# Feed-forward front, normalisation and q/k/v projections of a macaron layer reworked, with three waits moved

## What is computed

```python
x = x + 0.5 * ffn(_layernorm(x))
x = x + attn(_layernorm(x))
x = x + 0.5 * ffn(_layernorm(x))

def ffn(x):      # 8 experts of width 64, 2 chosen by row; a shared MLP of width 128
    logits = xf @ gate_w.T + lb_bias
    topw, topi = top_k(sigmoid(logits), 2); topw = topw / (topw.sum(-1) + 1e-8)
    for e in range(8):
        m = topi == e
        wmean = (topw * m).sum() / maximum(m.sum(), 1)
        out = out + where(m.any(-1)[:, None], _mlp(xf, e) * wmean, 0)
    return out + _mlp(x, shared)          # _mlp: silu(x @ gw.T) * (x @ uw.T) @ dw.T

def attn(x):     # 16 heads of 8, 4 key/value heads, causal, with a linear bias by position
    q, k, v = x @ Wq + bq, x @ Wk + bk, x @ Wv + bv
    return softmax(q @ k.T * scale + slopes * rel) @ v @ Wo + bo
```

## Time and profile before

| | |
|---|---|
| Median of 3 runs (lowest, highest) | 827.32 us (825.87, 828.84) |
| The profiled execution's own time | 826.89 us |
| Its span, first to last instruction | 824.9 us |
| Mean granted TensorE clock | 0.96 of 2.4 GHz |
| Busy: PE, DVE, ACT, POOL | 753.1, 592.5, 431.5, 69.7 us |
| Chain that ended last, shares | PE 63%, DVE 19%, issue 12%, ACT 3%, POOL 1% |

### The profile page before, as it was taken

How to read it: one execution, slowest core, us unless ns; L and a number is a source line. 1 busy time by engine, 2 the same in 40 slices (tenths; PEclk the granted TensorE clock), 3 DMA queues, 4 the chain that set the end, 5 groups by cost and what they waited for, 6 DMA issues and landing times.

```text
span 824.9 us, 15805 instructions
## 1 busy us (share of the span) xinstructions
PE 753.1 (91%) x5508; PEld 329.2 (40%) x5508; DVE 592.5 (72%) x1913; ACT 431.5 (52%) x626; POOL 69.7 (8%) x83
## 2 busy tenths in 40 slices
PE   3979998775799999999999999999998879899998
PEld 2623333332234344444444444444443655233343
DVE  4875332777899999999999999999993377433301
ACT  3432323333337687676876768767677434223211
POOL 2200000444400000000000000000000021000000
PEclk9979999999769999999999999999999989699999
DMA  4201000153401010110101101011000000000012
GB/s 128 67 0 15 0 1 0 49 160 95 133 13 34 20 34 18 34 35 22 32 18 35 34 21 32 18 35 35 22 14 2 1 1 1 0 1 0 0 39 64
DMA packets 33068, 26.08 MB, mean 32 GB/s; under 512 B 5707, under 2 KB 32331, under 8 KB 32997
## 3 DMA queue, kind: packets, MB, share of 16 engines
q1 hardware_dynamic: 32996, 25.15, 10.7%
HBM read 14.62 MB, written 10.26 MB: 30 GB/s over the span
## 4 chain that ended last, share of the span: by engine, by line
PE 63%; DVE 19%; issue 12%; ACT 3%; POOL 1%; SPq 0%; DMA 0%; DVEq 0%; ACTq 0%; POOLq 0%
PE ps L964 57%; DVE mx L853 8%; PE ps L969 5%; DVE xn L659 3%; DVE mx L846 1%; ACT h_all L580 1%; POOL rstd L421 1%; DVE stats L647 1%; PE ps L1012 1%; DVE x L802 1%; DVE h_all L846 1%; DVE mv L651 1%; DMA x<-in_x 0%; SPq L310 0%; DVE wb L874 0%
## 5 line engine op out<-in xcount | busy, mean ns | idle before, releaser
L580 ACT ACTIVATE h_all<-ps 128x1024 f32<-128x1024 f32 (+3 forms) x384 | 291.1, 811 | 118.4 <-PE ps L964 115.0
L853 DVE TENSOR_REDUCE mx<-ps 128x1 f32<-128x512 f32 (+2 forms) x352 | 222.6, 681 | 8.5 <-PE ps L964 5.9
L964 PE MATMUL ps<-ks,xnT_all 57*128 57x512 bf16 (+3 forms) x768 | 180.3, 336 | 10.7 <-DVE mx L846 5.3
L964 PE MATMUL ps<-h_all,vb 128*32 128x512 f32 (+3 forms) x1536 | 163.0, 498 | 0.6 <-ACT osb L569 0.6
L964 PE MATMUL ps<-xnT_all,ks 59*128 59x512 bf16 (+3 forms) x768 | 158.4, 330 | 3.7 <-ACT h_all L580 3.4
L846 DVE CUSTOM_DVE_ANT_0 h_all<-ps,mask_w 128x384 bf16<-128x384 f32 (+1 forms) x256 | 148.9, 618 | 2.1 <-issue 0.3
L670 DVE TENSOR_TENSOR h_all<-ps,sg 128x512 f32<-128x512 f32 (+1 forms) x80 | 55.1, 689 | 107.9 <-PE ps L964 71.3
L964 PEld LDWEIGHTS ps<-ks,xnT_all 57*128 57x128 bf16 x768 | 56.7, 94 | 141.3 <-DVE mx L846 66.1
L964 PE MATMUL ps<-cb 64*128 64x64 bf16 (+3 forms) x1216 | 111.8, 214 | 0.0
L495 ACT ACTIVATE sg<-ps 128x512 f32<-128x512 f32 x80 | 47.6, 598 | 106.3 <-PE ps L964 106.3
L964 PEld LDWEIGHTS ps<-cb 64*128 64x128 bf16 x1216 | 79.8, 96 | 16.7 <-issue 0.3
(11 more groups left out here) (123 smaller groups left out, 627.3 us busy)
## 6 DMA issues: line engine op xcount, KB each, us to landing
xnT_all<-q_scr SPq DMA_DIRECT2D x64, 96.0 KB
q_scr<-qp SPq DMA_DIRECT2D x8, 384.0 KB, 2.7
ks<-k_scr SPq DMA_DIRECT2D x64, 48.0 KB
x<-in_x SPq DMA_DIRECT2D x8, 256.0 KB, 2.9
q_scr<-qp SPq DMA_DIRECT2D x8, 256.0 KB, 2.9
out<-x SPq DMA_DIRECT2D x8, 256.0 KB, 2.3
xnT_all<-bias_scr SPq DMA_DIRECT2D x64, 18.0 KB
q_scr<-qp SPq DMA_DIRECT2D x8, 128.0 KB, 2.3
```

Of the source, the lines that this page charges most:

```text
L580: act.activation(pr[:, (NSTEP * i + s) % PR_BUFS, p:HPG:SLOTS, lo:HALF], ps[:, b:b + 2, lo:HALF], ACT.Exp)\
L853: dve.tensor_reduce(m, src, AX.X, V.max).then_inc(a_out, 1)
L964: return pe.matmul(o, l, r, start=start, stop=stop, skip_group_check=True)
```

## The change

- **Loops.** Every group and batch loop is written out; the hardware loops are gone.
- **Loads.** x of groups 0 and 1 first, then wg and wu, then the other x loads without a wait between them. The small loads (ident, gate_w, lb, rank) go on ACT's queue. The masks, esel, slopes and qpos come later under `s_const`; ACT's conversion of them moves to behind group 6 of the first front, DVE's slope parts to behind the choice.
- **Normalised rows.** DVE writes a shift, -mean times rstd, in one small operation; ACT writes xn in four ACTIVATEs with scale and bias columns (24 groups in all).
- **Front.** One copy of the transposes in place of two. The shared expert of groups 4 to 7 (`LATE_SHARED`) is done behind the last gate on PE, behind the sigmoid on ACT, and within the choice on DVE. The mask transposes of group 0 come ahead of the first two expert tiles. maskT and esel have 128 rows, zeros below the eighth.
- **Projections.** v is projected straight into rows (four matmuls with xnT as weights, 32 columns), k into four 32-partition blocks of 128 columns (four matmuls with 32-column weights); `v_T` is gone. k's split moves from POOL to DVE, on 128 x 128. SP stores k with six DMAs in place of three (nine in all for each group).
- **Order.** `xn_T` is issued behind `down` instead of within it; DVE takes the values of group c-1 in place of c-2.

```diff
-STORES = 2 * len(RUNS)
+STORES = len(RUNS) + PARTS
+LATE_SHARED = GROUPS - 4
 def over_groups(body):
+    for c in range(GROUPS):
+        body(c, c % 2, c == 0, c == GROUPS - 1)
...
-                    sp.dma_start(k_scr[b, :, r:r + products, n], kp[:, par, 0:products]).then_inc(dw, 16)
+                    for m in range(products):
+                        sp.dma_start(k_scr[b, :, r + m, n].rearrange("k (t n) -> t k n", t=GT), kp[:, par, m])\
+                            .then_inc(dw, 16)
...
+            def ln_apply(c, par, s_nm, s_T, s_xn):
+                act.wait_ge(s_nm, c + 1)
+                after(act, s_T, c)
+                for t in range(GT):
+                    ins = act.activation(xn[:, t, :], x[:, c * GT + t, :], ACT.Identity, bias=shift[:, par, t:t + 1],
+                                         scale=rstd[:, par, t:t + 1])
+                ins.then_inc(s_xn, 1)
...
                 def front(c, par, first, last):
                     act.wait_ge(f.T, c + 1)
-                    after(act, f.U, c - 1)
-                    act.activation(xnT[:, par, :], bank(7 * par), copy).then_inc(f.xT, 1)
                     act.activation(xnT_all[:, c, :], bank(7 * par), copy).then_inc(f.xA, 1)
-                    if not first:
+                    if not last:
+                        ln_apply(c + 1, 1 - par, f.nm, f.T, f.xn)
+                    if 0 < c <= LATE_SHARED:
                         silu(c - 1, 1 - par)
+                    if load_constants and c == GROUPS - 2:
+                        constants()
...
                 act.wait_ge(f.lg, GROUPS)
                 act.activation(sc, lg, ACT.Sigmoid).then_inc(f.sig, 1)
+                for c in range(LATE_SHARED, GROUPS):
+                    silu(c, c % 2)
...
                     if qkv and not first:
                         qk(c - 1, 1 - par)
+                    if qkv:
+                        ln_apply(c, par, f.nm2, f.Tb, f.xn2)
...
+            def ln_shift(c, par, s_rs, s_xn, s_nm):
+                after(dve, s_xn, c - 1)
                 dve.wait_ge(s_rs, c + 1)
-                for t in range(GT):
-                    ins = dve.tensor_scalar(xn[:, t, :], x[:, c * GT + t, :], mv[:, par, t, 0:1],
-                                            rstd[:, par, t:t + 1], V.subtract, V.mult)
+                dve.scalar_tensor_tensor(out=shift[:, par, :], in0=mv[:, par, :, 0], scalar=-1.0, in1=rstd[:, par, :],
+                                         op0=V.mult, op1=V.mult).then_inc(s_nm, 1)
...
                     if not last:
                         statistics(c + 1, 1 - par)
-                    ln_apply(c, par, f.rs, f.T, f.xn)
+                    ln_shift(c, par, f.rs, f.xn, f.nm)
                     if c >= 2:
                         finish(c - 2, par)
...
                     mm(bank(5), wq[:, :], xnT[:, par, :]).then_inc(f.Q, 1)
-                    mm(ps[0:2 * KVH * DH, 6, :], wkv[:, :], xnT[:, par, :]).then_inc(f.K, 1)
+                    for t in range(GT):
+                        ins = mm(ps[:, 7, w * t:w * t + w], xnT[:, par, t * P:(t + 1) * P], wkv[:, w:2 * w])
+                    ins.then_inc(f.V, 1)
+                    for t in range(GT):
+                        ins = mm(ps[w * t:w * t + w, 6, 0:P], wkv[:, 0:w], xnT[:, par, t * P:(t + 1) * P])
+                    ins.then_inc(f.K, 1)
```

More of the change, by code:

```diff
@@ L206, in macaron @@
         rstd = sb("rstd", [P, 2, GT])
+        shift = sb("shift", [P, 2, GT])
         idle = sb("idle", [P, 4 + HPG])
@@ L265, in macaron @@
         s_late = sem("s_late")
-        s_x0 = sem("s_x0")
+        s_const = sem("s_const")
+        s_x = [sem(f"s_x{c}") for c in range(GROUPS)]
         s_init = sem("s_init")
@@ L373, in _ @@
                 load_stack(1, 1, 1, half)
-            with sp.Fori(1, BATCH) as b:
+            for b in range(1, BATCH):
                 store_parts(2 * b, b, 0)
@@ L396, in _ @@
             od = out.rearrange("(c t p) f -> c p t f", t=GT, p=P)
-            with sp.Fori(0, GROUPS) as c:
+            for c in range(GROUPS):
                 sp.wait_ge(f2.x, c + 1)
@@ L422, in rsqrt @@
                 pool.wait_ge(rs_sem, c + 1)
[L424 to L434, removed]
-                if not first:
-                    split(c - 1, 1 - par)
-            over_groups(pool, lambda c, par, first, last: rsqrt(c, par, f1.ve, f1.xn, f1.rs))
+            over_groups(lambda c, par, first, last: rsqrt(c, par, f1.ve, f1.xn, f1.rs))
             clear_keys()
             pool.wait_ge(f1.U, HT * GROUPS)
-            over_groups(pool, down_body)
-            split(GROUPS - 1, 1)
+            over_groups(lambda c, par, first, last: rsqrt(c, par, f1.ve2, f1.xn2, f1.rs2))
             pool.wait_ge(s_late, 16 * len(late_loads))
@@ L469, in _ @@
             pool.wait_ge(o_bo, BO_PARTS)
-            over_groups(pool, lambda c, par, first, last: rsqrt(c, par, f2.ve, f2.xn, f2.rs))
+            over_groups(lambda c, par, first, last: rsqrt(c, par, f2.ve, f2.xn, f2.rs))
         @block.scalar
@@ L475, in _, with constants @@
             copy = ACT.Copy
[L476 to L479, removed]
+            for dst, name in small_loads:
+                act.dma_start(dst[:, :], dram[name]).then_inc(s_small, 16)
+            def constants():
+                act.wait_ge(s_init, 2)
+                act.wait_ge(s_const, 16 * len(const_loads))
+                act.activation(cb[:, :, :], c128[:, 0:7 * P].rearrange("p (a n) -> p a n", n=P), copy).then_inc(s_cb, 1)
+                act.activation(mask_w[:, HALF - P:HALF], c128[:, 7 * P:8 * P], copy)
+                act.activation(esel[0:EXPERTS, :], esel_f[:, :], copy).then_inc(s_cb, 1)
             def stack_constants():
@@ L708, in choose, with shared @@
                 def choose():
+                    def shared(c):
+                        hidden(c, c % 2, c, MT)
                     dve.wait_ge(f.sig, 1)
@@ L717, in choose @@
                     mask(0, 0)
+                    for c in range(LATE_SHARED + 2, GROUPS):
+                        shared(c)
                 def mask(c, par):
@@ L942, in out_proj @@
                 residual(1, 1)
-                with dve.Fori(1, BATCH - 1) as b:
+                for b in range(1, BATCH - 1):
                     gather(2 * b + 2, b + 1, 0, 0)
@@ L1032, in routed_tiles, with down @@
                             .then_inc(f.tops, 1)
-                over_groups(pe, front)
-                up(GROUPS - 1, 1, MT, xnT[:, 1, :], None)
-                pe.wait_ge(f.xA, GROUPS)
-                over_groups(pe, routed_tiles)
+                over_groups(front)
+                for c in range(LATE_SHARED, GROUPS):
+                    up(c, c % 2, MT, xnT_all[:, c, :], None)
+                pe.wait_ge(s_cb, 2)
+                over_groups(routed_tiles)
             def ffn_down(f, qkv):
-                def down(c, par, transpose=0):
+                def down(c, par, transpose=False):
                     after(pe, f.yT, c - 1)
                     for i in range(HT):
-                        if transpose > 1 and i == 2:
-                            v_T(c - 3)
-                        if transpose and i == HT // 2 + 1:
-                            xn_T(c - 2)
                         ins = mm(bank(par), wds[:, i, :], h_all[:, c, i, :], start=(i == 0), stop=(i == HT - 1))
                     ins.then_inc(f.Y, 1)
+                    if transpose:
+                        xn_T(c - 2)
                 def project(c, par):
@@ L1069, in body @@
                     if not last:
-                        down(c + 1, 1 - par, 0 if first or not qkv else 1 if isinstance(c, int) and c == 1 else 2)
+                        down(c + 1, 1 - par, qkv and not first)
                     pe.wait_ge(f.yT, c + 1)
```

190 lines of the change are left out of this document (86 added, 104 removed).

## The result

The kernel after takes **807.78 us** (median of 4 runs, 805.28 to 809.99), beside 827.25 for the kernel before on the same chip: a ratio of 0.976, 95% interval 0.973 to 0.980. The prediction said 813.5, within 804 to 823, and faster at 0.86. Number and side were right, the number in part by luck: the reasons held only in part, and the largest term of the result had been priced at nothing.

A forecast was written before the change was run, and what follows sets the result against it. It saw the first down stage bound by a loop through xn and POOL's k split, the fronts by PE. First step -1.4, down stage -11.8, second step -0.3 summed to -13.5, giving 813.5 us, range 804 to 823.

The forecast's parts named there:

- choice and clock: Choice and experts: choice -1.2, third tile +1.8, then -3.3 and -5.8 in the two steps if the clock holds.
- the fronts: Both fronts: a new loop of 4.4 a group for 3.1; +1.3 at the first last gate, +4.9 in the second step.
- the down stage: First down stage: period 8.0 against 10.3, ending xn's wait and POOL's slowing; -14.3 to the last residual add.
- attention: From the last residual add to the first scores: DVE's added work and the wait for k cost +2.5.
- The failed step: Experts: 128 rows instead of 8 in the mask matmul change nothing, since its columns set the time.
- the slowing by POOL: First down stage: DVE's four xn take 3.79 while POOL splits k, 1.11 where POOL did nothing; this ends.
- the one SP stall: First down stage: SP's stores are late once, holding ACT's queue, so PE stalls 2.5 once.
- if the shorter idle keeps the clock: -3.3 and -5.8: Experts, third tile to group 2's mask transposes: 9.6 at 2.4 GHz, where it took 12.9 and 15.4.
- the rival of the clock at the front's end: Front's end: the clock drops and shared tiles run partly at 1.2 GHz; 3.6 a step, 821 us; chance 0.17.
- POOL holding the shift: Fronts: POOL's rsqrt delays DVE's shift by 1.0 us for each of eight groups; 822 us; chance 0.12.
- k's stores: Down stage: k stores bound SP, deciding against the kernel from about 1.3 each; 837 us at 1.5; chance 0.04.
- The early loop: Fronts: the loop closes earlier and the period stays 3.1, eight groups less 1.3; 804 us; chance 0.08.

The follow-up runs named there:

- e1: The changed kernel with the mask matmul back on 8 rows of weights and mask: 823.63 us, ratio 0.994 to the kernel before.
- e11: The kernel before, with only k's three split operations moved from POOL to DVE: 821.57 us, ratio 0.991.
- e7: The changed kernel with DVE writing xn in the down stage, ACT still in the fronts: 805.28 us, ratio 0.972 to the kernel before.
- e6: The changed kernel with silu(c-1) ahead of xn(c+1) in ACT's front: 805.01 us, ratio 0.971 to the kernel before.
- e10: The changed kernel with DVE writing all xn and the shared tiles of groups 4 to 6 back in the front: 790.96 us, ratio 0.953 to the kernel before.

## Why the prediction was right, and where it wasn't

By the spans of the profiled executions the two kernels differ by -16.8; the sum of the prediction was -13.5. (By the medians it is -19.5.) In the two expert stretches the mask matmul brings -16.3 that I didn't have (-8.0 and -8.3, after against e1). The other steps miss by +13.0 together: choice and clock +4.1 and +3.3 (e1 against before: +1.4 and -1.9, where I had -2.7 and -5.2), the fronts +0.5 and +1.2, the down stage +0.7, attention +3.5, the end -0.3. The two nearly cancel, and that is luck. The kernel that I had priced, with the mask's columns alone setting its time, is e1: 823.63, just past the far end of the range, and worth 0.6%, not 1.6%. (e1's attention is 4.2 shorter than the changed kernel's, so the steps other than the mask miss by 9.1 there.)

- **The failed step: "128 rows instead of 8 in the mask matmul: nothing, its columns set the time."** The columns set its duration in the record, not what its neighbours lose. The starts in the kernel before already showed it: the gate matmul takes 0.86 to the next start with a full matmul behind it (726.52 to 727.38) and 0.96 with the mask behind it (724.29 to 725.25). From the mask to the next matmul it is 0.31, and 0.22 with 128 rows (716.07 to 716.29). My own sum held the price too: a tile of 2.25 less four instructions of 0.43 leaves 0.53 for a mask matmul that I had put at 0.2 one sentence earlier. I priced the instruction and didn't read the gaps around it.
- **Down stage: size right (-13.6 for -14.3), cause half right.** I named two things, the wait for xn and the slowing by POOL. e11 and e7 show that only POOL's k split mattered: with it gone DVE has room for xn, and everything else in the stage together adds 1.8 of 13.6. The estimates of xn on ACT (1.6; 1.65), the period (8.0; 7.91) and the one SP stall (2.5; PE 3.3) held. The terms of PE's work add up to 7.6, not 7.5, which changes nothing here.
- **Fronts: right.** +1.8 and +6.1 for +1.3 and +4.9, a period of 4.44 for 4.4, with the chain that was read from the two queues; e6 opened it where it was said to close. First transposes at 9.05 for 9.1. In the second step the transposes of group 3 come 14.0 behind the first ones where 13.0 was worked out; its terms add up to +4.8, not +4.9.
- **Choice and clock: the clock right behind the choice, the time wrong.** The clock after the choice was kept (1.00 in 52 to 60, for 0.55 before), as "if the shorter idle keeps the clock: -3.3 and -5.8" asks. It was lost ahead of it: 0.50 from 23.0 to 29.8 and from 33.2 to 46.9, for 1.00 before. This was the rival of the clock at the front's end, at 0.17, and half of it came true beside the forecast, not in place of it. From the gate's end to the mask transposes it takes 9.6 and 8.9 where 7.9 was worked out: DVE's two multiplies in the choice wait 1.8 and 1.1 for shared matmuls that ran at 1.2 GHz. The tiles themselves end in time; PE waits 0.27 for the mask. From there to the third tile it takes 4.9 as worked out (4.95). The larger miss lies behind that: to the mask transposes of group 2 it takes 11.7 and 10.3, for 9.6 by PE's work alone, at a clock of 1.00. In the first step DVE is the bound there. Windows view of that stretch, after:

```profile
56.79:68.53 11.74, 9.42 (x26) 3.44 (x26) 11.28 (x23) 3.42 (x6) 0.00 (x0) 1.00 0.00 0
```

PE waits 1.37 of it for DVE's multiply and 0.80 for the mask; the same stretch takes 11.7 in e1, with 8 rows. The stretch before held 11.94 of DVE's work (52.73 to 65.62), which I hadn't added up. e10 shows that the move of the shared tiles is worth nothing once xn is on DVE.

- **Attention: +6.0 for +2.5.** First scores came 35.3 behind the last add for 31.7, +3.6 for the +2.5. Windows view from the last add to the first scores, before and then after:

```profile
205.43:237.14 31.71, 25.89 (x82) 7.85 (x82) 28.99 (x96) 6.66 (x10) 10.07 (x10) 0.66 0.31 95
```
```profile
186.98:222.32 35.34, 29.34 (x105) 11.39 (x103) 28.53 (x99) 7.79 (x15) 2.64 (x4) 0.50 0.29 85
```

The other 2.3 lie between the first scores and the last add of attention's output (427.6 for 425.3), which no edit touches. They go with the granted clock, a mean of 0.98 for 0.99: 1.00 is reached 8.9 us behind the first scores, for 3.1 before. In e1 that part takes 423.5.

All the other kernels take 458.8 to 463.1 for the attention, in their profiled executions, where the kernel before took 457.0. What picks the value within that span isn't settled: no kernel was tried that keeps PE busy across ACT's wait for the store, behind which the clock fell in the changed kernel (wq's two instructions at 180.73 take 2.08, the price of 1.2 GHz).
- **Rivals that fell.** POOL holding the shift: DVE's shift took 0.16, and POOL's rsqrt starts behind it (24.28 and 24.50), not ahead. The rule of the Trainium skill's page "SBUF — State Buffer" ("SBUF: two separate sides") therefore wasn't tested on the shift: the two didn't meet. Where xn met k's split they took turns (last section), as such a lock would have it; xn beside the rsqrt shows none. k's stores: 0.50 to 0.66 each, far from 1.3. The early loop, which I put at 804, is 813.4 less 10.4, so 803.0. Loops written out: no stretch shows anything of it, but nothing was run with that alone.

## What to carry over

Read the starts of the neighbours of a small matmul, not its duration: one whose weights have 64 rows or fewer, or 8 columns, between full ones costs 0.2 to 0.3 more than its columns, and zeros up to 128 make that vanish for a memset. Before work is moved off an engine because that engine waits or runs slowly, find what slows it: moving the small disturber (k's split off POOL) did nearly all of what moving the large victim (xn to ACT) was meant to do, and the move of the victim cost 16 us, 13.6 of it in the fronts, where the other engine's queue closed a loop. Price each stretch by every engine's work in it: behind the choice PE had 9.6 and DVE over 11. When a total comes out as forecast, still cut both traces at the same events; here the cut showed errors of 13 and 16 that hid each other by luck.

## What the hardware showed that I had not expected

- A bf16 matmul with few rows between fp32 ones of 128 costs 0.30, with a step between 64 and 96 rows: 8 and 64 rows cost the same (2.23 from gate to gate), 96 and 128 the same (1.93). Below the step the weight loads beside it aren't hidden behind the matmul ahead. Width does the like: 8 columns for 128 cost 0.2 for each set of transposes.
- Three wide POOL operations of 1.15 beside DVE turned four xn of 1.11 into 3.79; the four-element rsqrt beside the same xn didn't. They don't share, they take turns: the first three xn operations end 0.09 behind one POOL operation each (159.84, 160.95 and 162.17, for POOL's 159.75, 160.86 and 162.08), and the fourth, alone, takes 0.33. Taking the three away shortened the period by 2.3, though DVE took their work over.
- A shorter stage may be followed by a slower clock: from the last add to the first scores the granted clock is 0.50 in the changed kernel and 0.66 before. What decides it isn't shown.
